# Window attention block on one core: K and Q projected ahead of the first MLP layer, their low parts taken ahead of x's statistics

## The chip, the cores and the metric

The kernel runs on one core of one Trainium2 chip. The metric is the time of one execution in microseconds (us) of device time. Names of engines: PE is TensorE (matmuls), PEld its weight loads, DVE is VectorE, ACT is ScalarE, POOL is GpSimd, SP is SyncE, which here only issues DMAs.

## The reference

One block of a Swin transformer on x of 32 images of 56 x 56 tokens with 128 channels, in float32: windows of 7 x 7 tokens, shifted by 3, 16 heads of 8 channels, an MLP with 512 hidden channels. Cut to what matters:

```
y = layernorm(x, norm1_g, norm1_b); y = roll(y, (-3, -3)); yw = windows of 7 x 7 tokens of y
q, k, v = split(yw @ qkv_w.T + qkv_b)              # 16 heads of 8
attn = softmax(q * 8**-0.5 @ k.T + bias + mask)     # bias by relative position, mask where the roll wraps
o = roll(attn @ v @ proj_w.T + proj_b, (3, 3))
x = x + o
h = layernorm(x, norm2_g, norm2_b)
out = x + gelu(h @ fc1_w.T + fc1_b) @ fc2_w.T + fc2_b
```

## The kernel before

A step of the work is a band of 7 rows of a pair of images: 16 windows, 784 tokens. There are 128 steps (`STEPS`), and the engines work through turns `t` of -2 to 130; each turn holds pieces of several steps, so that attention of step t, K, Q and maximum logits of step t + 1, statistics of x of step t + 2, the output projection of step t - 1, and the MLP of steps t - 2 and t - 3 share one turn. Nothing is scheduled by a tool: each engine's program is written out by hand in the order in which it runs, each instruction waits for semaphores, and a wait that is not yet met holds up all that stands behind it on that engine.

The order of a turn in which all pieces exist (t from 2 to 126), as far as the change and the prediction touch it:

- PE: transposes of z2 (L838, step t - 2) and of z1 (L846, step t + 1), the transpose of the maxima (L749), the first three token rows of the second MLP layer (`fc2(t - 3, 0, i)`, L821), chunks 0 and 1 of the first MLP layer (`fc1`, L805: six matmuls a chunk, into PSUM banks 2 and 3 or 4 and 5), K and then Q (L867: six matmuls each, K into banks 0 and 1, Q into banks 6 and 7), chunks 2 and 3 of fc1, the spread of the softmax reciprocals over channels (L881), V (L895, 24 matmuls), the output projection (L904), and then eight windows of logits (L771, L776), maximum logits (L741), attention times V (L791) and the rest of fc2.
- ACT: `h_hi` (L449), `yT_hi` (L464, four pieces), the table for gelu, gelu of chunks 0 and 1 (L438), `k_hi` and `q_hi` (L484), gelu of chunks 2 and 3, the table for exp, half of V (L500), then the exponentials (L421).
- DVE: `h_lo` (L600), the negated maxima (L607), `yT_lo` (L617, L621), reciprocals of the softmax sums (L630), `finish(t - 3, 0)` (L581), which frees bank 7, then `norm1(t + 2)` (statistics of x: seven at L521, seven at L527), `k_lo` and `q_lo` (L641), the division (L657), the other half of V (L672, L687), the residual (L681), the row maxima (L589).
- SP issues in this order: softmax sums, x of step t + 2 (L206), the attention's output, two pieces of the negated maxima (L246), the reciprocals' rows (L281), two more pieces of L246, the four `mx_k` (L296) and `mx_q` (L300) copies for the maximum logits, the output, 15 copies into `st_k` and `st_q` (L315, L318), x again for the residual.

Every f32 value that goes into a 16-bit matmul is split into a high part (a cast) and a low part (the difference), so K needs `yT_hi` and `yT_lo`, and `k_hi`, `k_lo` are made by ACT and DVE in turn from the same PSUM banks. The waits that matter:

```
pe.wait_ge(s_y_lo, n + 1)                            # ahead of K; n = t + 1
if bank == 6 and exists(t - 3):
    pe.wait_ge(s_fin, 2 * (t - 3) + 2)               # ahead of Q: finish(t - 3, 0) has read bank 7
pe.wait_ge(s_h_lo, n + 1)                            # fc1 chunk 0
pe.wait_ge(s_gelu, CH * n + c - 1)                   # fc1 chunk c = 2, 3: gelu of chunk c - 2 has read the banks
pe.wait_ge(s_lo, 2 * (t + 1) + 1)                    # spread: k_lo has read banks 0 and 1
pe.wait_ge(s_lo, 2 * (t + 2))                        # V: q_lo has read banks 6 and 7
dve.wait_ge(s_x, loads(n, edge(n)))                  # norm1: x of step t + 2 has landed
```

In the last turns (t of 127 and more) there is no step t + 1 any more, so K and Q are absent there, and from t = 126 on there is no `norm1`.

Of the kernel before, what the change touches and what calls it, by code (L numbers as in the profile page):

```python
# [71 lines left out]
def swin_block_kernel(nc, x, wqT, wkT, wvT, wvpT, wpT, w1T, w2T, cols, rows, table_k, table_q, ident, eye,  # L72
# [11 lines left out]
    with ctx:  # L84
# [63 lines left out]
        def tokens_of(bank):  # L148
            return ps[:, bank:bank + 2, :].rearrange("p b (i c) -> p (b i) c", c=C)
# [34 lines left out]
        def exists(n):  # L184
            return 0 <= n < STEPS

        def past(n, k):
            return n > k

        def loads(n, edge):  # L190
            return 64 * (n + 1) - 32 * EDGE if edge else 32 * (n + 1)
# [212 lines left out]
        @block.scalar  # L404
        def _(act):
            act.wait_ge(s_w, 16 * N_W)

            nc.scalar.mul(w_q, w_q, HD ** -0.5).then_inc(s_inita, 1)
            nc.scalar.mul(col[:, BQ:BQ + 1], col[:, BQ:BQ + 1], HD ** -0.5).then_inc(s_inita, 1)
            act.wait_ge(s_inita, 2)  # L410

            def load_table(function):

                nc.scalar.activation(scrap[:, :], col[0:1, 0:1], function)  # L414

            def exp_pair(n, w):
                if w >= 4 or past(n, 0):
                    act.wait_ge(s_pv, NU * n + w // 2 - 1)
                act.wait_ge(s_st, NW * n + w + 1)
                b = 2 + 2 * (w % 2)  # L420
                nc.scalar.activation(probs[0:KP, w % 4, :].rearrange("p (b c) -> p b c", b=2),  # L421
                                     ps[0:KP, b:b + 2, 0:HB * WT], ACT.Exp).then_inc(s_exp, 1)

            def copy_pv(n, u):
                act.wait_ge(s_pv, NU * n + u + 1)
                if u == 0 and past(n, 0):
                    act.wait_ge(s_o_dma, N_O * n)
                    act.wait_ge(s_sum_dma, N_SUM * n)
                nc.scalar.activation(pv_sb[:, :, 2 * u * WT:2 * (u + 1) * WT],  # L429
                                     ps[:, 6, 0:NG * 2 * WT].rearrange("p (g q) -> p g q", g=NG),  # L430
                                     ACT.Copy).then_inc(s_pv_sb, 1)

            def gelu(n, c):
                if c == 0 and past(n, 0):
                    act.wait_ge(s_fc2, 2 * n)
                act.wait_ge(s_fc1, CH * n + c + 1)
                bank = 2 + 2 * (c % 2)
                nc.scalar.activation(hid[:, c, :].rearrange("p (b q) -> p b q", b=2), ps[:, bank:bank + 2, 0:HT],  # L438
                                     ACT.Gelu, bias=col[:, BF + c:BF + c + 1], scale=1 / W_SCALE).then_inc(s_gelu, 1)

            def body(t, edge, odd):
                if exists(t - 1):
                    copy_pv(t - 1, NU - 1)
                n = t - 2
                if exists(n):
                    act.wait_ge(s_t2, n + 1)
                    if past(n, 0):
                        act.wait_ge(s_fc1, CH * n)
                    nc.scalar.activation(h_hi[:, :].rearrange("p (i c) -> p i c", c=TP),  # L449
                                         tokens_of(2)[:, 0:WS, 0:TP], ACT.Copy).then_inc(s_h_hi, 1)  # L450
                n = t + 1
                if exists(n):

                    act.wait_ge(s_t1, n + 1)
                    if past(n, 1):
                        act.wait_ge(s_v, 2 * (n - 1))
                    else:
                        act.wait_ge(s_initp, 1)
                    src = tokens_of(0)[:, 0:WS, 0:TP].rearrange("p i (m c) -> p i m c", m=2)
                    dst = yT_hi[odd(1)][:, :, :, 0:WT].rearrange("p w m (i j) -> p w m i j", i=WS)  # L460
                    last_w = NW - 1
                    kept = WS - SS
                    def put(o, a):
                        return nc.scalar.activation(o, a, ACT.Copy)  # L464
                    for im in range(2):
                        put(dst[:, 0:last_w, im, :, :].rearrange("p w i j -> p i w j"),
                            src[:, :, im, SS:SS + last_w * WS].rearrange("p i (w j) -> p i w j", j=WS))
                    put(dst[:, last_w, :, :, 0:kept].rearrange("p m i j -> p i m j"),
                        src[:, :, :, W - kept:W])
                    put(dst[:, last_w, :, :, kept:WS].rearrange("p m i j -> p i m j"),  # L470
                        src[:, :, :, 0:SS]).then_inc(s_y_hi, 1)
                if exists(t - 2):
                    load_table(ACT.Gelu)
                    gelu(t - 2, 0)
                    gelu(t - 2, 1)
                n = t + 1
                if exists(n):

                    if past(n, 0):
                        act.wait_ge(s_mx_dma, N_MX * n)  # L480
                        act.wait_ge(s_st_dma, N_ST * n)
                    for j, (hi, bank, b) in enumerate(((k_hi, 0, BK), (q_hi, 6, BQ))):
                        act.wait_ge(s_qk, 2 * n + j + 1)
                        nc.scalar.activation(hi[:, :, :, :].rearrange("p w m q -> p m w q"),  # L484
                                             ps[:, bank:bank + 2, 0:BT].rearrange("p m (w q) -> p m w q", w=NW),
                                             ACT.Identity, bias=col[:, b:b + 1]).then_inc(s_hi, 1)
                if exists(t - 2):
                    gelu(t - 2, 2)
                    gelu(t - 2, 3)
                if exists(t):  # L490
                    load_table(ACT.Exp)
                n = t
                if exists(n):
                    if past(n, 0):
                        act.wait_ge(s_pv, NU * n)
                    else:
                        act.wait_ge(s_init, 2)
                    for b in range(2):
                        act.wait_ge(s_v, 2 * n + b + 1)
                        nc.scalar.activation(v_place(1, b), v_made(1, b), ACT.Copy).then_inc(s_vown_b, 1)  # L500
                if exists(t):
                    for w in range(NW):
                        exp_pair(t, w)
                        if w % 2 == 0 and w > 0:
                            copy_pv(t, w // 2 - 1)

            turns(body)


        @block.vector  # L510
        def _(dve):
# [18 lines left out]
            def norm1(n, edge):  # L530
                dve.wait_ge(s_x, loads(n, edge(n)))
                if past(n, 0):
                    dve.wait_ge(s_z1, n)
                stats(x_in, st1, (0, WS)).then_inc(s_st1, 1)
                aggregate(n, st1, s_st1, mv1, s_ln1)
# [59 lines left out]
            def body(t, edge, odd):  # L595
                n = t - 2
# [4 lines left out]
                n = t  # L601
# [7 lines left out]
                n = t + 1  # L609
# [16 lines left out]
                n = t - 1  # L626
# [3 lines left out]
                    nc.vector.reciprocal(sums[:, :, :], sums[:, :, :]).then_inc(s_rsum, 1)  # L630
                if exists(t - 3):
                    finish(t - 3, 0, edge)
                n = t + 2
                if exists(n) and n != 0:
                    norm1(n, edge)
                n = t + 1
                if exists(n):
                    for j, (hi, lo, bank, b) in enumerate(((k_hi, k_lo, 0, BK), (q_hi, q_lo, 6, BQ))):
                        dve.wait_ge(s_hi, 2 * n + j + 1)
                        for im in range(2):  # L640
                            last = nc.vector.scalar_tensor_tensor(  # L641
                                lo[:, :, im, :], ps[:, bank + im, 0:BT].rearrange("p (w q) -> p w q", w=NW),
                                col[:, b:b + 1], hi[:, :, im, :], ALU.add, ALU.subtract)
                        last.then_inc(s_lo, 1)
                n = t - 1
                if exists(n):

# [18 lines left out]
                n = t  # L666
# [6 lines left out]
                n = t - 1  # L673
# [10 lines left out]
                n = t  # L684
# [3 lines left out]
                for w in range(NW):  # L688
                    if exists(t + 1):
                        row_maxima(t + 1, w)  # L690
                    n = t - 1
# [14 lines left out]
        def _(pe):  # L706
# [119 lines left out]
            def body(t, edge, odd):  # L826
                if exists(t - 1):
                    pv(t - 1, NU - 1)
                n = t - 2
# [10 lines left out]
                n = t + 1  # L840
# [9 lines left out]
                if exists(t - 3):  # L850
                    for i in range(*FC2_PARTS[0]):
                        fc2(t - 3, 0, i)
                if exists(t - 2):
                    fc1(t - 2, 0)
                    fc1(t - 2, 1)
                n = t + 1
                if exists(n):
                    pe.wait_ge(s_y_lo, n + 1)
                    high, low = ([y[odd(1)][:, :, im, 0:WT] for im in range(2)] for y in (yT_hi, yT_lo))
                    for w_hi, w_lo, bank in ((wk_hi, wk_lo, 0), (wq_hi, wq_lo, 6)):  # L860
# [6 lines left out]
                                last = mm(ps[:, bank + im, 0:BT], ww[:, :], yy[im], start=(k == 0), stop=(k == 2))  # L867
                        last.then_inc(s_qk, 1)
                if exists(t - 2):
                    fc1(t - 2, 2)  # L870
                    fc1(t - 2, 3)
                n = t - 1
# [11 lines left out]
                n = t  # L884
# [14 lines left out]
                n = t - 1  # L899
# [79 lines left out]
```

## Time and profile before

| | |
|---|---|
| median of 3 runs | 4095.21 us (4090.11 to 4104.3) |
| the profiled execution | 4095.41 us, span 4093.6 us |
| PE busy | 3947.3 us, 96% of the span |
| DVE, ACT, POOL busy | 70%, 65%, 49% |
| mean granted TensorE clock | 0.995 |

The span runs from the first to the last instruction of one profiled execution; the profiled execution's own time is 1.8 us more. A share of busy time is that of the whole span. Matmuls are pipelined, and the length shown for one (0.33 us for 392 columns) is more than the distance from one to the next (0.165 us); a group of two in the rows has one start, the next group's start tells the pace. A turn lasts some 31 us.

### The profile page before, as it was taken

Reading aid. Unit: us, or ns where it says so; the run is one execution under the profiler, and the core shown is the slowest. Engines: PE = TensorE matmul, PEld = TensorE weight load, DVE = VectorE, ACT = ScalarE, POOL = GpSimd, SP = SyncE. Lnnn points to the kernel's source line nnn. Section 1 sums busy time; section 2 is a strip of 40 time slices with the busy share of each in tenths; the row PEclk is TensorE's granted clock in tenths of the full one; section 3 lists DMA queues with packets and bytes.
Section 4 is the critical chain, followed back from the end, with each engine's and each line's share of the span. In section 5 each row is a group of like instructions: output and inputs, shape, how many; then the busy total and the mean of one; then the engine's idle time right before and its main releaser. Section 6 shows DMA issues by size and latency. Waiting matters only on the chain. (4 is left out here: it accounts for less than half of the span.)

```text
span 4093.6 us, 168809 instructions
## 1 busy us (share of the span) xinstructions
PE 3947.3 (96%) x72080; PEld 3111.1 (76%) x72080; DVE 2855.1 (70%) x7453; ACT 2674.9 (65%) x3712; POOL 2002.3 (49%) x3476
## 2 busy tenths in 40 slices
PE   3899999999999999999999999999999999999998
PEld 2677777777777777777777777777777777777776
DVE  6677677677767777776776776777777667677764
ACT  1666666666666666666766666666666666666664
POOL 4454545445455454544544544454454445445453
PEclk8999999999999999999999999999999999999999
DMA  2333333333333333333333333333333333333332
GB/s 77 100 108 115 109 109 112 110 105 112 114 106 110 113 111 110 111 113 105 112 114 105 110 114 110 109 111 108 108 109 117 106 109 112 112 105 109 112 109 60
DMA packets 609568, 441.49 MB, mean 108 GB/s; under 512 B 142083, under 2 KB 608371, under 8 KB 608819
## 3 DMA queue, kind: packets, MB, share of 16 engines
q1 hardware_dynamic: 608355, 428.88, 35.6%
q8 instruction: 569, 9.32, 1.0%
q0 software_dynamic: 464, 1.81, 0.2%
q14 instruction: 180, 1.47, 0.1%
HBM read 106.14 MB, written 51.46 MB: 38 GB/s over the span
## 5 line engine op out<-in xcount | busy, mean ns | idle before, releaser
L589 DVE TENSOR_REDUCE neg_max<-ps 113x16 f32<-113x784 f32 x1024 | 995.9, 973 | 760.7 <-PE ps L741 760.5
L421 ACT ACTIVATE probs<-ps 113x784 f32<-113x784 f32 x1024 | 844.6, 825 | 858.4 <-PE ps L776 855.7
L821 PE MATMUL ps<-w,hid 128*112 128x128 f32 x7168 | 933.5, 279 | 1.9 <-ACT hid L438 1.0
L821 PEld LDWEIGHTS ps<-w,hid 128*112 128x112 f32 x7168 | 818.4, 177 | 81.9 <-issue 79.4
L776 PE MATMUL ps<-st_q,st_k 128*49 128x196 f16 x8192 | 696.2, 249 | 0.0
L771 PE MATMUL ps<-bias,eye_k 106*64 106x392 f16 x4096 | 686.5, 331 | 0.0
L438 ACT ACTIVATE hid<-ps,col 128x784 f32<-128x784 f32 x512 | 468.1, 915 | 165.4 <-PE ps L805 144.2
L741 PE MATMUL ps<-mx_k,mx_q 128*49 128x196 f16 x8192 | 544.2, 253 | 31.7 <-DMA mx_q<-q_hi 20.0
L350 POOL TENSOR_SCALAR ve<-mv 112x7 f32<-112x7 f32 x256 | 54.4, 212 | 1048.4 <-DVE mv L527 903.1
L776 PEld LDWEIGHTS ps<-st_q,st_k 128*49 128x49 f16 x8192 | 446.9, 105 | 122.0 <-issue 0.5
L372 POOL TENSOR_SCALAR r_hi<-sums 128x98 f16<-128x98 f32 x128 | 36.5, 285 | 897.9 <-DVE sums L630 897.9
L791 PE MATMUL ps<-probs,v_own 113*32 113x49 f32 x32768 | 464.4, 209 | 1.8 <-issue 1.5
L791 PEld LDWEIGHTS ps<-probs,v_own 113*32 113x32 f32 x32768 | 393.2, 110 | 83.6 <-issue 82.8
L741 PEld LDWEIGHTS ps<-mx_k,mx_q 128*49 128x49 f16 x8192 | 313.1, 103 | 152.1 <-DMA mx_q<-q_hi 33.1
L361 POOL TENSOR_SCALAR x_in<-x_in,rs,nm 112x128 f32<-112x128 f32 x896 | 389.5, 451 | 13.5 <-POOL nm L356 0.4
L361 POOL TENSOR_SCALAR z<-x,rs,nm 112x128 f32<-112x128 f32 x896 | 388.5, 449 | 13.4 <-POOL nm L356 0.3
L352 POOL TENSOR_TENSOR rs<-ve,half 112x7 f32<-112x7 f32 x256 | 380.4, 1486 | 21.3
L429 ACT ACTIVATE pv_sb<-ps 128x392 f32<-128x392 f32 x512 | 255.6, 499 | 203.9 <-PE ps L791 192.4
L414 ACT ACT_TABLE_LOAD x253 | 324.6, 1283 | 4.5
L521 DVE BATCH_NORM_STATS2 st<-x_in 112x6 f32<-112x128 f32 x896 | 185.9, 279 | 201.8 <-DMA x_in<-in_x 201.8
L384 POOL TENSOR_TENSOR x_res<-x_res,proj_b 112x896 f32<-112x896 f32 x128 | 267.2, 2088 | 10.3
L391 POOL TENSOR_TENSOR x_b<-x,fc_b 112x896 f32<-112x896 f32 x128 | 267.1, 2087 | 5.6 <-DVE y_out L581 5.6
(109 smaller groups left out, 6502.4 us busy)
## 6 DMA issues: line engine op xcount, KB each, us to landing
st_k<-k_hi SPq DMA_DIRECT2D x256, 196.0 KB
st_q<-q_hi SPq DMA_DIRECT2D x1024, 49.0 KB
oT_raw<-pv_sb SPq DMA_DIRECT2D x256, 196.0 KB, 3.6
x_in<-in_x SPq DMA_DIRECT2D x224, 196.0 KB
x_res<-in_x SPq DMA_DIRECT2D x224, 196.0 KB
out_y<-y_out SPq DMA_DIRECT2D x224, 196.0 KB
mx_k<-k_hi SPq DMA_DIRECT2D x512, 49.0 KB
mx_q<-q_hi SPq DMA_DIRECT2D x128, 196.0 KB
```

Source lines behind the costliest of these rows:

```text
L352: nc.gpsimd.tensor_tensor(rs[:, :], ve[:, :], half[:, :], ALU.pow).then_inc(s_rs, 1)
L361: last = nc.gpsimd.tensor_scalar(z[:, i, :], src[:, i, :], rs[:, i:i + 1], nm[:, i:i + 1], ALU.mult, ALU.add)
L384: nc.gpsimd.tensor_tensor(x_res[:, :, :], x_res[:, :, :], proj_b[:, :].unsqueeze(1).to_broadcast([TP, WS, C]), ALU.add).then_inc(s_xres, 1)
L414: nc.scalar.activation(scrap[:, :], col[0:1, 0:1], function)
L421: nc.scalar.activation(probs[0:KP, w % 4, :].rearrange("p (b c) -> p b c", b=2), ps[0:KP, b:b + 2, 0:HB * WT], ACT.Exp).then_inc(s_exp, 1)
L438: nc.scalar.activation(hid[:, c, :].rearrange("p (b q) -> p b q", b=2), ps[:, bank:bank + 2, 0:HT], ACT.Gelu, bias=col[:, BF + c:BF + c + ...
L589: nc.vector.tensor_reduce(neg_max[0:KP, :, :, w].rearrange("p e g -> p g e"), ps[0:KP, 0:2, :].rearrange("p b (g c) -> p (b g) c", g=2)[:, ...
L741: last = mm(group(im, 0, g, 256), mx_q[edge(n)][:, g, span], mx_k[:, g, :, span], start=True, stop=True)
L771: mm(ps[HP * im:HP * (im + 1), bank + b, 0:HB * WT], eye_k[0:BIAS_ROWS, kind, im, :], bias[0:BIAS_ROWS, b, :], start=True, stop=False)
L776: last = mm(group(im, bank, g, EQ * WT), st_k[par][:, g, span], st_q[par][:, :, g, span], start=False, stop=(g % 2 == 1))
L791: last = mm(ps[32 * r:32 * r + VC, 6, first:first + WT], v_own[0:KP, w, h, :], probs[0:KP, w % 4, h * WT:(h + 1) * WT], start=True, stop=True)
L821: last = mm(ps[0:TP, 7, (i - first) * C:(i - first + 1) * C], hid[:, c, i * TP:(i + 1) * TP], w_2[:, c, :], start=(c == 0), stop=(c == CH ...
```

## The change

On PE, K and Q are computed ahead of all four chunks of fc1 and no longer between chunks 1 and 2. On ACT, `k_hi` and `q_hi` come ahead of all four gelus. On DVE, `k_lo` and `q_lo` come ahead of `norm1`. All waits stay with their instructions; no instruction is added or removed, and the orders on SP and POOL are the same as before.

```
--- before.py
+++ after.py
@@ scalar
                 if exists(t - 2):
                     load_table(ACT.Gelu)
-                    gelu(t - 2, 0)
-                    gelu(t - 2, 1)
                 n = t + 1
                 if exists(n):
...
                                              ACT.Identity, bias=col[:, b:b + 1]).then_inc(s_hi, 1)
                 if exists(t - 2):
+                    gelu(t - 2, 0)
+                    gelu(t - 2, 1)
                     gelu(t - 2, 2)
                     gelu(t - 2, 3)
@@ vector
                 if exists(t - 3):
                     finish(t - 3, 0, edge)
-                n = t + 2
-                if exists(n) and n != 0:
-                    norm1(n, edge)
                 n = t + 1
                 if exists(n):
                     for j, (hi, lo, bank, b) in enumerate(((k_hi, k_lo, 0, BK), (q_hi, q_lo, 6, BQ))):
...
                         last.then_inc(s_lo, 1)
+                n = t + 2
+                if exists(n) and n != 0:
+                    norm1(n, edge)
@@ tensor
                     for i in range(*FC2_PARTS[0]):
                         fc2(t - 3, 0, i)
-                if exists(t - 2):
-                    fc1(t - 2, 0)
-                    fc1(t - 2, 1)
                 n = t + 1
                 if exists(n):
                     pe.wait_ge(s_y_lo, n + 1)
...
                         last.then_inc(s_qk, 1)
                 if exists(t - 2):
+                    fc1(t - 2, 0)
+                    fc1(t - 2, 1)
                     fc1(t - 2, 2)
                     fc1(t - 2, 3)
```

PE, from the end of fc2's first part on, before (L867 is K and Q, L805 is fc1; what stands in brackets is the semaphore waited for):

```order
L821 MATMUL ps<-w,hid 112x128 x11
L805 MATMUL ps<-h_hi,w_hi 128x392 [waits h_low_ready]
L805 MATMUL ps<-h_hi,w_hi 128x392
L805 MATMUL ps<-h_lo,w_hi 128x392 x2
L805 MATMUL ps<-h_hi,w_lo 128x392 x2
L805 MATMUL ps<-h_hi,w_hi 128x392 [waits exp_done]
L805 MATMUL ps<-h_hi,w_hi 128x392
L805 MATMUL ps<-h_lo,w_hi 128x392 x2
L805 MATMUL ps<-h_hi,w_lo 128x392 x2
L867 MATMUL ps<-yT_hi,wk_hi 128x392 [waits y_low_ready]
```

PE at the same place of the changed kernel, whose line for K and Q is L864:

```order
L821 MATMUL ps<-w,hid 112x128 x11
L864 MATMUL ps<-yT_hi,wk_hi 128x392 [waits y_low_ready]
L864 MATMUL ps<-yT_hi,wk_hi 128x392
L864 MATMUL ps<-yT_lo,wk_hi 128x392 x2
L864 MATMUL ps<-yT_hi,wk_lo 128x392 x2
L864 MATMUL ps<-yT_hi,wq_hi 128x392 [waits y_ready,neg_maxT_ready]
L864 MATMUL ps<-yT_hi,wq_hi 128x392
L864 MATMUL ps<-yT_lo,wq_hi 128x392 x2
L864 MATMUL ps<-yT_hi,wq_lo 128x392 x2
L805 MATMUL ps<-h_hi,w_hi 128x392 [waits h_low_ready]
```

Chunks 0 and 1 of fc1, twelve matmuls, stood between fc2 and K; now K follows fc2, and all four chunks of fc1 follow Q without anything between chunk 1 and chunk 2.

DVE, from `finish` to the division, before:

```order
L581 TENSOR_TENSOR y_out<-ps,x_b 112x384 [waits fc2_done]
L521 BN_STATS st<-x_in 112x6 [waits z1_ready,x_loaded]
L521 BN_STATS st<-x_in 112x6 x6
L527 BN_AGGR mv<-st 112x2 [waits stats1_done]
L527 BN_AGGR mv<-st 112x2 x6
L641 SCALAR_TENSOR_TENSOR k_lo<-ps,col,k_hi 128x8x49 [waits qk_high_ready]
L641 SCALAR_TENSOR_TENSOR k_lo<-ps,col,k_hi 128x8x49
L641 SCALAR_TENSOR_TENSOR q_lo<-ps,col,q_hi 128x8x49 [waits qk_high_ready]
L641 SCALAR_TENSOR_TENSOR q_lo<-ps,col,q_hi 128x8x49
L657 TENSOR_TENSOR oT<-oT_raw,ps 128x7x49 [waits projected,r_spread,o_in]
```

DVE at the same place of the changed kernel, whose line for the low parts is L638:

```order
L581 TENSOR_TENSOR y_out<-ps,x_b 112x384 [waits fc2_done]
L638 SCALAR_TENSOR_TENSOR k_lo<-ps,col,k_hi 128x8x49 [waits qk_high_ready]
L638 SCALAR_TENSOR_TENSOR k_lo<-ps,col,k_hi 128x8x49
L638 SCALAR_TENSOR_TENSOR q_lo<-ps,col,q_hi 128x8x49 [waits qk_high_ready]
L638 SCALAR_TENSOR_TENSOR q_lo<-ps,col,q_hi 128x8x49
L521 BN_STATS st<-x_in 112x6 [waits z1_ready,x_loaded]
L521 BN_STATS st<-x_in 112x6 x6
L527 BN_AGGR mv<-st 112x2 [waits stats1_done]
L527 BN_AGGR mv<-st 112x2 x6
L657 TENSOR_TENSOR oT<-oT_raw,ps 128x7x49 [waits projected,r_spread,o_in]
```

The wait for x's load (`x_loaded`) stood ahead of the low parts and now stands behind them.

## Rows read from the trace of the kernel before

**Rows 1.** The page: busy time of the engines, and TensorE's granted clock in tenths.

```profile
PE 3947.3 (96%) x72080; PEld 3111.1 (76%) x72080; DVE 2855.1 (70%) x7453; ACT 2674.9 (65%) x3712; POOL 2002.3 (49%) x3476
PEclk8999999999999999999999999999999999999999
```

**Rows 2.** Waits: who waited for whom, us in total, times, longest.

```profile
PE ps L895 <- DVE q_lo L641: 24.2, 55, 2.2
PE ps L741 <- DMA mx_q<-q_hi: 20.0, 24, 4.3
PE ps L881 <- DVE k_lo L641: 14.5, 26, 2.8
PE ps L881 <- DMA r_rows<-r_lo: 2.0, 3, 0.9
DVE st L521 <- DMA x_in<-in_x: 201.8, 128, 2.8
DVE sums L630 <- DMA sums<-pv_sb: 4.6, 9, 1.2
```

**Rows 3.** Timeline of PE in one turn: start us, us, instructions.

```profile
1478.69 0.49 PE L805 MATMUL ps<-h_hi,w_hi 128*128 128x392 f16 x2
...
1480.68 0.50 PE L867 MATMUL ps<-yT_hi,wk_hi 128*128 128x392 f16 x2
...
1481.70 0.50 PE L867 MATMUL ps<-yT_hi,wq_hi 128*128 128x392 f16 x2
...
1482.72 0.49 PE L805 MATMUL ps<-h_hi,w_hi 128*128 128x392 f16 x2
...
1484.81 0.50 PE L881 MATMUL ps<-r_rows,sel 32*128 32x392 f16 x2
1485.24 0.23 PE L895 MATMUL ps<-wv_hi,yT_hi 128*128 128x128 f16 x1
...
1486.62 1.78 PE L904 MATMUL ps<-w_p,oT 128*112 128x128 f32 x14
```

**Rows 4.** Timeline of DVE and ACT in the same turn.

```profile
1478.32 0.34 DVE L621 TENSOR_TENSOR yT_lo<-ps,yT_hi 128x56 f16<-128x56 f32 x2
...
1479.22 0.50 DVE L581 TENSOR_TENSOR y_out<-ps,x_b 112x384 f32<-112x384 f32 x1
...
1484.02 1.15 DVE L641 SCALAR_TENSOR_TENSOR q_lo<-ps,col,q_hi 128x392 f16<-128x392 f32 x2
1485.40 1.16 DVE L657 TENSOR_TENSOR oT<-oT_raw,ps 128x343 f32<-128x343 f32 x4 [0.23 <-issue]
...
1477.35 1.28 ACT L414 ACT_TABLE_LOAD   x1
...
1479.95 1.85 ACT L438 ACTIVATE hid<-ps,col 128x784 f32<-128x784 f32 x2 [1.10 <-PE ps L805]
1481.98 0.93 ACT L484 ACTIVATE k_hi<-ps,col 128x784 f16<-128x784 f32 x1 [0.19 <-PE ps L867]
```

**Rows 5.** Timeline of DVE and PE in a turn with a late load of x.

```profile
2474.16 1.45 DVE L521 BATCH_NORM_STATS2 st<-x_in 112x6 f32<-112x128 f32 x7 [2.82 <-DMA x_in<-in_x]
...
2478.39 0.23 PE L895 MATMUL ps<-wv_hi,yT_hi 128*128 128x128 f16 x1 [0.49 <-DVE q_lo L641]
```

**Rows 6.** Timeline of PE's fc1 in a turn near the end, without K and Q.

```profile
4027.41 0.49 PE L805 MATMUL ps<-h_hi,w_hi 128*128 128x392 f16 x2
...
4029.63 0.51 PE L805 MATMUL ps<-h_hi,w_hi 128*128 128x392 f16 x2
```

**Rows 7.** Timeline of PE and DVE near the start, where K waited for yT_lo.

```profile
83.79 0.34 DVE L621 TENSOR_TENSOR yT_lo<-ps,yT_hi 128x56 f16<-128x56 f32 x2
...
84.19 0.84 PE L867 MATMUL ps<-yT_hi,wk_hi 128*128 128x392 f16 x2 [2.24 <-DVE yT_lo L621]
```

**Rows 8.** SP: its waits, and its timeline in the turn of rows 3.

```profile
SPq L294 <- ACT k_hi L484: 6.5, 2, 4.7
...
1483.54 2.92 SPq L296 DMA_DIRECT2D mx_k<-k_hi  x4
```

More of the change, by code:

```diff
@@ L473, in body @@
                     load_table(ACT.Gelu)
-                    gelu(t - 2, 0)
-                    gelu(t - 2, 1)
                 n = t + 1
@@ L487, in body @@
                 if exists(t - 2):
+                    gelu(t - 2, 0)
+                    gelu(t - 2, 1)
                     gelu(t - 2, 2)
@@ L632, in body @@
                     finish(t - 3, 0, edge)
-                n = t + 2
-                if exists(n) and n != 0:
-                    norm1(n, edge)
                 n = t + 1
@@ L644, in body @@
                         last.then_inc(s_lo, 1)
+                n = t + 2
+                if exists(n) and n != 0:
+                    norm1(n, edge)
                 n = t - 1
@@ L852, in body @@
                         fc2(t - 3, 0, i)
-                if exists(t - 2):
-                    fc1(t - 2, 0)
-                    fc1(t - 2, 1)
                 n = t + 1
@@ L869, in body @@
                 if exists(t - 2):
+                    fc1(t - 2, 0)
+                    fc1(t - 2, 1)
                     fc1(t - 2, 2)
```

## The prediction

> **What bounds the kernel now.** I read the page first: PE is busy 96% of the span, the next engine 70% [rows 1]. So only time in which PE waits, or is made to wait, counts. The view of waits says where the rest is: in the steady turns PE waits for `q_lo` ahead of V (24.2 us), for the copies of K and Q that the maximum logits need (20.0 us), for `k_lo` ahead of the spread (14.5 us) and for the rows of the reciprocals (2.0 us) [rows 2]. The first, third and last sum to 40.7 us; over the 125 turns in which all pieces exist (t = 2 to 126) that is 0.33 us a turn. This is all that the change can win at that place.
>
> Why PE waits there is seen in a turn with a late load [rows 5]. DVE stood 2.82 us in front of `norm1` until x landed; the low parts queued behind it, and V began 0.49 us late after a spread that was late too. DVE waits for that load in nearly every turn, 201.8 us in 128 [rows 2]; only where x is late enough does PE feel it. A turn with an early load shows the undisturbed pace [rows 3, 4]. I count its times from 1478.69, when fc2's first part is through and fc1 starts; call it 0. Then K starts at 1.99, Q at 3.01, chunk 2 of fc1 at 4.03, the spread at 6.12, V at 6.55, the projection at 7.93 [rows 3]. V is just not held up there: `q_lo` ends at 6.48 (1485.17). The other turns are late against this one by those 0.33 us on average.
>
> **The change, part by part.** No instruction is added or removed, so busy time stays and the sum is one of waits.
>
> *Removed.* `k_lo` and `q_lo` no longer stand behind `norm1` and its load, and they have both chunk pairs of fc1 as cover. The 24.2 and 14.5 us go: -38.7 us. If nothing else moved, the kernel would win 0.9%.
>
> *Added: K directly behind fc2.* Chunks 0 and 1 of fc1 took 1.99 us and covered the making of `yT_lo`. That ends at 1478.66 [rows 4], which is -0.03. The start of the kernel, where K did wait, shows that K's first matmul begins 0.06 us after `yT_lo` ends (84.13 to 84.19) [rows 7]. K thus starts at 0.03: +0.03 us. That is luck rather than cover: any lateness of `yT_lo` now counts in full.
>
> *Added: Q behind `finish`.* Q needs bank 7, which `finish(t - 3, 0)` reads until 1479.72, that is 1.03 [rows 4]. With 0.06 for the wake-up Q starts at 1.09, where K's end would allow 1.05 (K to Q is 1.02): +0.04 us. Chunk 0 of fc1 starts at 2.11.
>
> *Added: the four chunks in one piece.* Chunk 2 writes the banks that gelu 0 reads, and Q and K no longer stand between. The turns near the end have just this order: chunk 0 starts at 4027.41, chunk 2 at 4029.63, 2.22 us later where two chunks take 1.99 us [rows 3, 6]: +0.23 us. (The wait is gelu's length plus the delay from chunk 0's start to gelu's, 1.26 us by rows 3 and 4, against 1.99 us of matmuls.) Chunk 3 then waits for gelu 1, which ends some 0.94 us after gelu 0, while chunk 2 takes 1.0 us: nothing, or 0.02. So chunk 2 starts at 4.33, the spread 2.09 later [rows 3] at 6.42 to 6.44, and V another 0.43 later at 6.86.
>
> *Is DVE in time?* `k_hi` ends at 0.03 + 1.30 + 0.93 = 2.26, `q_hi` at 1.09 + 2.23 = 3.32, `q_lo` 1.15 later at 4.5 [rows 3, 4]. `norm1` follows, about 2.0 us (from its start to V 4.23 us, less two low parts of 1.1 each [rows 4, 5]). Its load has landed by then: the longest wait for x in the run is the 2.82 us of [rows 5], begun when `finish` was through, so at 1.03 + 2.82 = 3.85. `norm1` thus ends at 6.5, ahead of the division, which waits for the spread: 0.59 us from the spread's start to its own [rows 3, 4], 1.16 us for itself, 0.06 until the projection, 6.43 + 1.81 = 8.24 against 7.93. V's matmuls, 1.38 us at most [rows 3], end at 8.24 as well. **A changed turn is longer than the undisturbed one by 0.31 us**: 125 x 0.31 = +38.8 us.
>
> *The late sums.* DVE waits 4.6 us in nine turns for the sums ahead of the reciprocal [rows 2]. `finish` stands behind that, and Q now waits for `finish` without slack: up to +4.6 us. The 2.0 us for the reciprocals' rows stay.
>
> *SP and POOL.* Their orders don't change. SP reaches the copies of K at 1483.54, when `k_hi` (ended 1482.91) was done, and in the whole run it waited for `k_hi` only twice [rows 4, 8]. So an earlier K starts no transfer earlier: `mx_k`, `mx_q`, output and `st_k`, `st_q` leave at the same times within a turn, and the 20.0 us of waiting for `mx_q` are not won. In those 24 turns the landing sets the pace, and a V that is 0.31 us later costs nothing there, up to 24 x 0.31 = 7.4 us less. But in some of these the removed wait had been hidden in the same way, so I take nothing off and use the 7.4 us for the lower end. POOL's first normalization gets its statistics some 0.5 us later, far ahead of the next turn's transposes, which wait for it. ACT's last gelu ends 0.3 us later, and PE first waits for the exponentials behind it at the third window's logits; I take that as covered, and it is a part of rival B if it isn't.
>
> *ACT's table load.* It now stands right ahead of `k_hi`. It starts at 1477.35 and shows 1.28 us, and gelu 0 runs 2.60 us after the load's start, having waited for PE [rows 4]. `k_hi` would be asked for at 0.03 + 1.30 = 1.33 (1480.02), 1.39 us behind the load's end: by the rows it waits for nothing. The Trainium skill (ScalarE: Activation LUTs, "What ACT_TABLE_LOAD costs") says that a switch costs about 2.66 us, a drain included; an estimate by it frees ACT at 1480.01 with a small activation still ahead of `k_hi`, which would move `k_hi` by that one's length and gelu 0 by hundredths, about 2 us over the run. The row shows gelu at work earlier than that, so the row decides.
>
> **Sum.** -38.7 + 38.8 + 4.6 = +4.7 us, made against the profiled execution's own 4095.4 us, which is 0.2 us from the median: 4100 us. The expected gain is real, and is given back by three new small waits, the largest at chunk 2.
>
> **Rivals.**
> *A, as above, within 0.3%:* 4100 us, own range 4090 to 4108. Chance 0.66.
> *B, gelu comes late (slower).* By the sum `q_hi` ends at 1.09 + 1.30 + 0.93 = 3.32 and gelu 0 is asked for at 2.11 + 1.26 = 3.37: a margin of 0.05 us. Every 0.1 us by which K, `finish` or ACT is later than my readings moves chunk 2 of each turn by 0.1 us, 12.5 us over the run. With 0.15 us more a turn the time is 4119 us. It decides (over 0.3%) from 0.06 us a turn. For it speaks that three waits in series have no slack; against, that all of them recur with a constant length. Chance 0.18.
> *C, the copies profit (faster).* If K's and Q's copies landed earlier, the 20.0 us of [rows 2] would go too: 4080 us. Against it stands SP's order [rows 8]. Chance 0.06.
> *D, the new waits don't arise (faster).* Were PE's weight loads or the order of work able to hide the wait for gelu, 125 x 0.23 = 29 us would come off: 4071 us. The turns near the end speak against it. Chance 0.05.
> *E, the clock.* TensorE's granted clock is at the full level in all slices but the first [rows 1], with PE standing 2 us at a time in some turns [rows 2]. If more short halts took it to the lower level for fc1, K and Q, some 6 us of a turn would double, 750 us in all: 4850 us. The Trainium skill (TensorE: Matmul & The Clock Gate, "A second HAM failure mode: psum-queue depth-cycling") tells of a kernel whose frequent short halts between groups made the clock swing; by that rule this would be the case, but the trace doesn't bear it out, halts of this size are there already. Chance 0.01.
> *F, nothing at all moves,* since x mostly lands early enough: the removed 38.7 us are measured waits, so this ends where A ends. Chance 0.04.
>
> **Numbers.** What a measurement of this kernel can tell from no change is about 0.3%, 12 us. A's range lies mostly inside it; B reaches over it. The range from 4083 to 4117 us leaves out E, most of C and D, and the upper part of B, in all less than 2 in 10. Faster by over 0.3% 0.12 (C, D, a little of A), within 0.3% 0.68, slower 0.20 (B, E and the upper edge of A).
>
> **What will show it.** In the changed kernel's view of waits, `q_lo` ahead of V and `k_lo` ahead of the spread should be gone, DVE's wait for x in front of the statistics too (x landed while it made the low parts). PE's weight loads should wait for ACT's gelu ahead of L805 in nearly every turn. In a timeline, K should start within 0.1 us of fc2's end, chunk 2 should start 2.22 us after chunk 0, and the distance from fc2's end to V should be 6.86 us in nearly all turns, where it was 6.55 to 8. `mx_q` should be waited for as often as before. I am wrong if `yT_lo` or `finish` come later than here (K or Q start late), if chunk 2 waits for more than 0.3 us, or if the transfers change their times within a turn.

## The result: 0.4% slower, and the profile after

The changed kernel takes 4109.96 us (median of 9 runs, 4106.26 to 4116.73), the kernel before 4095.21 us (9 runs in the same comparison, 4084.42 to 4104.3). The ratio is 1.004, 95% interval 1.0028 to 1.0052: slower, by less than 15 us. The profiled execution has a span of 4104.5 us where the one before had 4093.6.

The first two rows are of the page of the changed kernel, the others of its view of waits:

```profile
PE 3994.1 (97%) x72080; PEld 3097.4 (75%) x72080; DVE 2857.1 (70%) x7453; ACT 2673.2 (65%) x3712; POOL 2002.2 (49%) x3476
PEclk9999999999999999999999999999999999999999
...
PEld ps L805 <- ACT hid L438: 79.6, 255, 0.8
...
PE ps L741 <- DMA mx_q<-q_hi: 7.3, 8, 4.5
PE ps L864 <- DVE y_out L581: 3.8, 10, 0.9
PE ps L880 <- DMA r_rows<-r_lo: 3.5, 3, 1.7
PE ps L894 <- DVE q_lo L638: 2.2, 1, 2.2
...
DVE st L521 <- DMA x_in<-in_x: 2.4, 1, 2.4
```

Against [rows 2]: V's wait for `q_lo` fell from 24.2 to 2.2 us, the spread's wait for `k_lo` is gone, and DVE stood before x's statistics for 2.4 us instead of 201.8. What the change is made for, it does. In its place PE's weight loads wait for ACT ahead of fc1, 255 times. PE's busy time rose by 47 us although it runs the same matmuls: short waits hide in it, since the length shown for a matmul (0.33 us) reaches beyond the start of the next (0.165 us later). The busy share says nothing here; the starts do.

Timeline of PE in an undisturbed turn of the changed kernel:

```profile
2105.99 0.51 PE L864 MATMUL ps<-yT_hi,wk_hi 128*128 128x392 f16 x2
...
2107.14 0.50 PE L864 MATMUL ps<-yT_hi,wq_hi 128*128 128x392 f16 x2
...
2108.16 0.49 PE L805 MATMUL ps<-h_hi,w_hi 128*128 128x392 f16 x2
...
2110.38 0.51 PE L805 MATMUL ps<-h_hi,w_hi 128*128 128x392 f16 x2
...
2112.48 0.50 PE L880 MATMUL ps<-r_rows,sel 32*128 32x392 f16 x2
2112.91 0.23 PE L894 MATMUL ps<-wv_hi,yT_hi 128*128 128x128 f16 x1
...
2114.29 1.78 PE L903 MATMUL ps<-w_p,oT 128*112 128x128 f32 x14
```

Timeline of DVE and ACT in the same turn:

```profile
2106.49 0.50 DVE L581 TENSOR_TENSOR y_out<-ps,x_b 112x384 f32<-112x384 f32 x1
2108.27 1.16 DVE L638 SCALAR_TENSOR_TENSOR k_lo<-ps,col,k_hi 128x392 f16<-128x392 f32 x2 [1.27 <-ACT k_hi L482]
2109.34 1.15 DVE L638 SCALAR_TENSOR_TENSOR q_lo<-ps,col,q_hi 128x392 f16<-128x392 f32 x2
2110.41 1.44 DVE L521 BATCH_NORM_STATS2 st<-x_in 112x6 f32<-112x128 f32 x7
...
2107.31 0.93 ACT L482 ACTIVATE k_hi<-ps,col 128x784 f16<-128x784 f32 x1 [1.19 <-PE ps L864]
2108.36 0.93 ACT L482 ACTIVATE q_hi<-ps,col 128x784 f16<-128x784 f32 x1
2109.41 1.85 ACT L438 ACTIVATE hid<-ps,col 128x784 f32<-128x784 f32 x2
2111.59 1.91 ACT L438 ACTIVATE hid<-ps,col 128x784 f32<-128x784 f32 x2 [0.33 <-PE ps L805]
2113.52 1.28 ACT L414 ACT_TABLE_LOAD   x1
2114.81 0.20 ACT L414 ACTIVATE scrap<-col 1x1 f32<-1x1 f32 x1
2115.02 2.12 ACT L500 ACTIVATE v_own<-ps 49x512 f32<-49x512 f32 x2
```

Counted from the end of fc2's first part (4.12 us after the turn's first transpose, here 2105.97), K starts at 0.02, Q at 1.17, chunk 0 at 2.19, chunk 2 at 4.41, the spread at 6.51, V at 6.94, the projection at 8.32. The undisturbed turn of before had V at 6.55 and the projection at 7.93 [rows 3]. For averages below I took the start of V in each of the 121 turns from 232 us to 3992 us, counted in the same way: 6.88 before, 6.99 in the changed kernel. In the changed kernel V starts within 0.03 us of 6.94 in 99 of these turns, and later than 7.0 in 17, at most at 7.90. Before, it started within 0.05 us of 6.55 in 42 turns, ahead of 6.93 in 83, and the latest was at 8.08. So most turns became longer, by up to 0.39 us, and the late ones became fewer.

Two averages behind V matter for the sum. From V to the first logits (L771) the changed kernel takes 3.10 us; before it was 3.09 us in an undisturbed turn, but 3.04 on average, since more than half of the turns took only 3.01 to 3.02 there. Why is not shown. The first logits thus start 0.17 us later than before on average (10.09 instead of 9.92), and 0.09 us of that is absorbed by the end of the turn.

### The profile page after: what moved, and what is told of

It reads as the page before. It is cut to its first block, busy times and chain, and to the rows that moved or that the text cites. A ratio compares the mean times of both kernels' runs of the same rounds, so it can differ in the third digit from the quotient of the medians.

```text
span 4104.5 us, 168809 instructions
## 1 busy us (share of the span) xinstructions
PE 3994.1 (97%) x72080; PEld 3097.4 (75%) x72080; DVE 2857.1 (70%) x7453; ACT 2673.2 (65%) x3712; POOL 2002.2 (49%) x3476
## 4 chain that ended last, share of the span: by engine, by line
PE 87%; SPq 3%; ACT 3%; DMA 2%; DVE 2%; issue 2%; POOL 0%; ACTq 0%; DVEq 0%; POOLq 0%
PE ps L821 20%; PE ps L741 12%; PE ps L791 10%; PE ps L805 9%; PE ps L776 9%; PE ps L771 9%; PE ps L864 6%; PE ps L903 5%; PE ps L894 4%; ACT hid L438 3%; PE ps L838 2%; PE ps L846 2%; PE ps L880 1%; SPq L296 1%; DMA mx_q<-q_hi 1%
## 5 line engine op out<-in xcount | busy, mean ns | idle before, releaser
L771 PE MATMUL ps<-bias,eye_k 106*64 106x392 f16 x4096 | 687.1, 331 | 0.0
L500 ACT ACTIVATE v_own<-ps 49x512 f32<-49x512 f32 x256 | 265.4, 1139 | 7.4 <-PE ps L894 5.7
```

What stands on the lines that cost most here:

```text
L771: mm(ps[HP * im:HP * (im + 1), bank + b, 0:HB * WT], eye_k[0:BIAS_ROWS, kind, im, :], bias[0:BIAS_ROWS, b, :], start=True, stop=False)
```

## The experiments

Times are medians; the kernel before ran beside them and had 4092.8 us in the first four, 4092.4 us in the others. The changed kernel's 4109.96 us is from the comparison above, where the kernel before had 4095.2 us, so a difference from it is good to some 3 us; the ratios to the kernel before are free of that.

### 1. What does Q wait for? `finish` ahead of the reciprocal

```
 (DVE, changed kernel)
+                if exists(t - 3):
+                    finish(t - 3, 0, edge)
                 n = t - 1
                 if exists(n):
                     dve.wait_ge(s_sum_dma, N_SUM * (n + 1))
                     nc.vector.reciprocal(sums[:, :, :], sums[:, :, :]).then_inc(s_rsum, 1)
-                if exists(t - 3):
-                    finish(t - 3, 0, edge)
```

> The changed kernel with one swap on DVE: the addition that frees PSUM bank 7 (finish, first part) ahead of the reciprocal instead of behind it. In the changed kernel Q's first matmul starts 1.14 us behind K's, where K's matmuls alone take 1.02; I had forecast 1.06. Theory (Q stands behind finish): the bank is free 0.65 us earlier, Q starts 1.02 to 1.04 us behind K, a turn is 0.10 to 0.12 us shorter, about 13 us less than the changed kernel (4097 us against 4110), less what the 0.5 us later reciprocals cost through SP's queue (mx_k and mx_q leave up to 0.5 us later). Rival (two waits in front of Q cost this time whether they are met or not): Q still starts 1.14 us behind K and the time is that of the changed kernel or more.

Measured: 4097.63 us (12 runs), 12.3 us less than the changed kernel; ratio to the kernel before 1.0007 (0.9996 to 1.0019). Timeline of PE and DVE:

```profile
2101.88 0.51 PE L864 MATMUL ps<-yT_hi,wk_hi 128*128 128x392 f16 x2
...
2102.91 0.50 PE L864 MATMUL ps<-yT_hi,wq_hi 128*128 128x392 f16 x2
...
2102.05 0.56 DVE L581 TENSOR_TENSOR y_out<-ps,x_b 112x384 f32<-112x384 f32 x1 [0.23 <-PE ps L821]
```

With bank 7 free at 2102.61, Q follows K after 1.03 us; in the changed kernel it was 1.15 (2105.99 to 2107.14). The rival falls: Q was held by `finish`. `mx_k` leaves 0.52 us later in this kernel on average, and the waits for `mx_q` rose from 7.3 to 15.0 us, yet the time fell by nearly all of the 13 us forecast. Both waits still stand ahead of Q here.

### 2. Does chunk 2 wait for gelu? Half-length gelus

```
 (ACT, changed kernel, in gelu)
+                nb = 1 if c < 2 else 2
-                nc.scalar.activation(hid[:, c, :]..., ps[:, bank:bank + 2, 0:HT],
+                nc.scalar.activation(hid[:, c, 0:nb * HT]..., ps[:, bank:bank + nb, 0:HT],
```

> The changed kernel with the gelus of chunks 0 and 1 done for the first half of their columns only (392 of 784; half of these two chunks' hidden values stays undone), so that each lasts some 0.6 us instead of 0.92. Theory (chunk 2 of the first MLP layer waits 0.23 us for gelu 0): chunk 2 starts 1.99 us behind chunk 0 instead of 2.22, chunk 3 another 1.0 us later, a turn is 0.25 us shorter, 31 us less than the changed kernel: 4079 us. Rival (the 0.23 us is not gelu's, but a cost of the order of the matmuls or of the weight loads): chunk 2 still starts 2.22 us behind chunk 0 and the time stays at 4110 us.

Measured: 4084.97 us (12 runs), 25 us less than the changed kernel; ratio to the kernel before 0.9978 (0.9966 to 0.999). The kernel leaves out half of the gelus of chunks 0 and 1, so its time is not one for the whole work. Timelines of PE and ACT:

```profile
2093.54 0.49 PE L806 MATMUL ps<-h_hi,w_hi 128*128 128x392 f16 x2
...
2095.53 0.49 PE L806 MATMUL ps<-h_hi,w_hi 128*128 128x392 f16 x2
...
2094.80 0.59 ACT L439 ACTIVATE hid<-ps,col 128x392 f32<-128x392 f32 x1
```

Chunk 2 starts 1.99 us behind chunk 0, as forecast, and the rival falls. V starts 0.25 us earlier on average, 31 us over 125 turns; 25 us of it reach the end. The waits for `mx_q` rose from 7.3 to 22.1 us in the profiles of the two: where that landing sets the pace, an earlier V only waits longer. That this is where the other 6 us went is likely, not shown.

### 3. The change on PE and ACT alone

The changed kernel with `norm1` back ahead of the low parts on DVE (the middle part of the diff undone).

> The change on PE and ACT alone; on DVE x's statistics stay ahead of the low parts, as before. Theory (the three new waits come from PE's and ACT's order, and DVE's order only decides whether a late x reaches PE): K, Q and the chunks start as in the changed kernel, but q_lo ends 4.2 us after x has landed, which in a quarter of the turns is later than the spread's end; V is 0.14 us later on average, 18 us over the changed kernel: about 4125 us, and the waits of V for q_lo are back in some 30 turns. Rival (DVE's order is what costs, for instance by the later statistics): the time falls below the changed kernel's 4110 us.

Measured: 4115.3 us (6 runs), ratio 1.0049 (1.0032 to 1.0065); 5 us above the changed kernel where 15 us were forecast, and the two intervals (the changed kernel's is 1.0028 to 1.0052) overlap. DVE waits for x again, 191.4 us, and V waits for `q_lo` in 15 turns (6.9 us), not 30. V starts at 7.05 of the turn on average, 0.06 us later than in the changed kernel. The waits came back as forecast, but at less than half the size. That DVE's half of the change wins time once K and Q are both early is not shown by these runs; if it does, it is little.

### 4. A version of my own: K first, Q left between chunks 1 and 2

```
 PE                          ACT                    DVE
 K                           k_hi                   reciprocal, finish
 fc1 chunks 0, 1             gelu 0, gelu 1         k_lo
 Q                           q_hi                   norm1(t + 2)
 fc1 chunks 2, 3             gelu 2, gelu 3         q_lo
 spread, V                                          division
```

> A version of my own: K ahead of the first MLP layer as in the change, but Q left between chunks 1 and 2 as before; ACT in the order k_hi, gelu 0, gelu 1, q_hi, gelu 2, gelu 3; on DVE k_lo, then x's statistics, then q_lo. Theory (the change loses by the gap between chunk 1 and chunk 2 being closed, and by Q standing right behind finish): chunk 2 follows Q without a wait, Q has chunks 0 and 1 as cover for finish, only K's 0.03 us is left; x's landing is waited for 1 us later in the turn than before, so V starts at 10.83 us of the turn on average (before 11.00, changed kernel 11.1) and the time is 4075 to 4080 us. Rival (x's landing reaches PE as much as before, or K's early place costs elsewhere): 4095 us or more.

Measured: 4069.77 us (6 runs), ratio 0.9947 (0.9929 to 0.9965): faster than both, by 23 us against the kernel before and some 40 us against the changed one, and 5 us below the time expected. Timelines of PE and DVE:

```profile
2086.54 0.51 PE L866 MATMUL ps<-yT_hi,wk_hi 128*128 128x392 f16 x2
...
2089.56 0.50 PE L866 MATMUL ps<-yT_hi,wq_hi 128*128 128x392 f16 x2
...
2090.59 0.49 PE L812 MATMUL ps<-h_hi,w_hi 128*128 128x392 f16 x2
...
2092.67 0.50 PE L892 MATMUL ps<-r_rows,sel 32*128 32x392 f16 x2
...
2088.81 1.16 DVE L641 SCALAR_TENSOR_TENSOR k_lo<-ps,col,k_hi 128x392 f16<-128x392 f32 x2 [1.28 <-ACT k_hi L478]
2089.89 1.44 DVE L526 BATCH_NORM_STATS2 st<-x_in 112x6 f32<-112x128 f32 x7
...
2091.86 1.13 DVE L641 SCALAR_TENSOR_TENSOR q_lo<-ps,col,q_hi 128x392 f16<-128x392 f32 x2
```

Nothing waits between K and the spread: 6.13 us, against 6.49 in the changed kernel (2105.99 to 2112.48). The statistics fill the time in which DVE would wait for `q_hi`, and begin 0.8 us later than before on average, late enough for nearly every landing of x. V starts at 6.60 on average.

### 5. The 0.08 us that were missing: one wait less ahead of Q

```
 (PE, changed kernel)
-                        if bank == 6 and exists(t):
-                            pe.wait_ge(s_negT, t + 1)
                         if bank == 6 and exists(t - 3):
                             pe.wait_ge(s_fin, 2 * (t - 3) + 2)
```

> The changed kernel with one of the two waits ahead of Q taken out: that for the negated maxima (DVE makes them ahead of yT_lo, for which K has waited already, so that nothing is left unguarded). In the changed kernel Q starts 0.14 us behind the end of finish, where every other waiting matmul starts 0.05 to 0.07 us behind what it waits for. Theory (the second wait instruction in front of Q costs 0.08 us, which my forecast lacked): Q starts 0.06 us behind finish, a turn is 0.08 us shorter, 10 us less than the changed kernel (4100 us against 4110). Rival (the 0.14 us is between the end of an addition that reads PSUM and PE, whatever PE waits for): Q still starts 0.14 us behind finish and the time stays at 4110 us.

Measured: 4098.4 us (12 runs), 11.6 us less than the changed kernel; ratio to the kernel before 1.0014 (1.0004 to 1.0024). Timelines of PE and DVE:

```profile
2100.54 0.51 PE L862 MATMUL ps<-yT_hi,wk_hi 128*128 128x392 f16 x2
...
2101.60 0.51 PE L862 MATMUL ps<-yT_hi,wq_hi 128*128 128x392 f16 x2
...
2101.05 0.49 DVE L581 TENSOR_TENSOR y_out<-ps,x_b 112x384 f32<-112x384 f32 x1
```

Q starts 0.06 us behind the end of `finish` (2101.54). In the changed kernel it is 0.15 us (2106.99 to 2107.14). The semaphore taken out had long been reached; having two waits instead of one still cost 0.08 to 0.09 us a turn. The rival falls.

What the second wait adds can be seen. The view of line 861 of the changed kernel, which is the wait for `finish`, has an instruction of PE's sequencer for weight loads (PEldq) of its own in 124 turns; in this experiment there is none. In the kernel before, line 877, the wait for `k_lo` ahead of the spread, has one too:

```profile
L861 PEldq EVENT_SEMAPHORE  x124: 51/51/51, 176.3 to 4008.5; - x124
...
L877 PEldq EVENT_SEMAPHORE  x126: 51/51/51, 117.6 to 4002.4; - x126
```

So of two waits one becomes an instruction of 51 ns, here the one that is met last, and the weight load with the other wait comes behind it. In experiment 1 the same instruction is there, but `finish` is done while K's matmuls still run, and Q starts 1.03 us behind K: then it costs nothing that can be seen. Whether the price would go if the two waits changed places, so that the one met last stood with the weight load, was not tested.

### 6. The change on DVE alone

> The change on DVE alone, PE and ACT in the order of before. Theory (the low parts can go ahead of x's statistics only because K and Q come earlier): k_lo and q_lo still wait for k_hi and q_hi and end at 10.6 us of the turn, the statistics follow until 12.65 us and hold up the division; the projection starts at 13.9 us instead of 12.4, and the time is about 4270 us. Rival (DVE's order alone wins the waits for q_lo and k_lo): V starts at 10.67 us in every turn and the time is about 4055 us.

Measured in one run: 4240.71 us, the profiled one, against 4092.4 us of the kernel before. Timelines of DVE and PE:

```profile
2178.99 1.15 DVE L638 SCALAR_TENSOR_TENSOR q_lo<-ps,col,q_hi 128x392 f16<-128x392 f32 x2
2180.06 1.44 DVE L521 BATCH_NORM_STATS2 st<-x_in 112x6 f32<-112x128 f32 x7
...
2182.02 1.13 DVE L657 TENSOR_TENSOR oT<-oT_raw,ps 128x343 f32<-128x343 f32 x4
...
2183.21 1.46 PE L904 MATMUL ps<-w_p,oT 128*112 128x128 f32 x11 [1.49 <-DVE oT L657]
```

V starts at 6.55 in nearly every turn, so the two waits are indeed won, and the projection pays 1.5 us for it. It is 30 us less than forecast: the division starts 1.96 us behind the statistics, which I had put at 2.05 with a start 0.1 us later, and the waits for `mx_q` fall from 20.0 to 5.1 us behind the later projection. The rival had V's start right and the time wrong.

### 7. K first, but x's statistics ahead of both low parts

> My version with K ahead of the first MLP layer and Q between chunks 1 and 2, but with x's statistics ahead of both low parts, as before the change. Theory (that version's 25 us come from DVE's order, which takes x's late landing off PE; K's early place is only what makes the order possible): q_lo ends 4.2 us after x has landed, V starts at 11.0 us of the turn on average, the time is that of the kernel before, 4090 to 4098 us. Rival (the early K is what wins): it stays at 4070 us.

Measured: 4091.54 us (12 runs), ratio 0.9991 (0.9978 to 1.0004): no change. PE waits for `q_lo` 18.9 us in 47 turns and for `k_lo` 5.8 us in 12: the waits of [rows 2] are back, if somewhat smaller. Against experiment 4 it differs in the place of `norm1` alone, and that is worth 22 us. The early K by itself wins nothing.

### 8. K first, and SP's copies of the maxima ahead of the reciprocals' rows

```
 (SP, version of experiment 4)
                     neg(n, (0, 1), odd(0))
+                    neg(n, (2, 3), odd(0))
 ...
-                n = t
-                if exists(n):
-                    neg(n, (2, 3), odd(0))
```

> My version with K first, and on SP all four copies of the negated maxima ahead of the reciprocals' rows, where SP stood idle for 0.4 us before. Theory (mx_k and mx_q leave when SP has come to them, not when K and Q are ready): they leave 0.4 to 0.5 us earlier in the turn, the maximum logits wait less for mx_q (0.1 us a turn before), while the reciprocals' rows land 0.8 us later but mostly still ahead of the spread: 4062 to 4067 us against 4070. Rival (the wait for mx_q comes from the load on the DMA queues, not from when the copies are issued, or the later rows hold up the spread): 4070 us or more.

Measured: 4078.94 us (8 runs), ratio 0.997 (0.9955 to 0.9986), 9 us more than experiment 4; the two intervals just overlap, so the size is uncertain. Two rows of its view of waits:

```profile
PE ps L890 <- DMA r_rows<-r_lo: 21.4, 32, 2.9
...
PE ps L746 <- DMA mx_q<-q_hi: 8.4, 8, 4.5
```

`mx_k` left only 0.2 us earlier on average (8.84 instead of 9.04 us after the turn's first transpose), and the reciprocals' rows landed 1.0 us later. The wait for `mx_q` fell from 14.1 to 8.4 us, and 21.4 us for the rows took its place, where experiment 4 had 3.8. V starts at 6.76 on average, where experiment 4 had 6.60. My theory was wrong in its last step: the rows had no such reserve. The first step held by less than half, 0.2 us of the 0.4 to 0.5 expected.

## Why the prediction was right, point by point

The range (4083 to 4117 us) held the time, and the likeliest value was 10 us low. The case that I held for likeliest, A, did not quite come: its own range ended at 4108 us, 2 us below the median. What came out, slower by a little over 0.3%, had a chance of 0.2. The waits of the forecast came where it put them; that its sum was this close is in part luck, since errors of both signs met in it, as is told below the list.

- *Removed, 38.7 us:* right for the waits. 2.2 of the 24.2 us stay, in one turn, and the 14.5 us are gone. But they were worth less than they show: between V and the first logits the kernel before was 0.06 us a turn quicker (3.04 against 3.10 us), which gives back some 7 us over the run.
- *K directly behind fc2, +0.03 us:* right, K starts at 0.02.
- *Q behind `finish`, +0.04 us:* this is the mis-sized term of the sum. The mechanism was right (experiment 1), but Q starts at 1.17, not at 1.09, +0.12 us: I took 0.06 us for the wake-up, read from a matmul with one wait, and Q has two (experiment 5). The difference is 0.08 x 125 = 10 us. Without it (experiment 5) the kernel is 6.0 us above the one before, where the sum had 4.7. The price stood in the trace of before, in the very turn of [rows 5], from which I read only the wait in front of V. The spread has two waits, V has one:

```profile
2476.14 1.13 DVE L641 SCALAR_TENSOR_TENSOR k_lo<-ps,col,k_hi 128x392 f16<-128x392 f32 x2
2477.19 1.15 DVE L641 SCALAR_TENSOR_TENSOR q_lo<-ps,col,q_hi 128x392 f16<-128x392 f32 x2
...
2477.42 0.49 PE L881 MATMUL ps<-r_rows,sel 32*128 32x392 f16 x2 [0.92 <-DVE k_lo L641]
```

  `k_lo` ends at 2477.27 and the spread starts 0.15 us later; `q_lo` ends at 2478.34 and V starts at 2478.39, 0.05 us later. The spread has this distance in 31 turns of the kernel before.
- *Four chunks in one piece, +0.23 us:* right to the hundredth. Chunk 2 starts 2.22 us behind chunk 0, and experiment 2 shows that it is gelu's length. The last turns of the kernel, which run the changed order already, were a sound place to read it [rows 6].
- *DVE in time:* right. `q_lo` ends at 2110.49, 4.5 us into the turn; the statistics are through before the division, and only one turn waits for x.
- *The turn:* an undisturbed one 0.31 us longer was forecast, 0.39 was measured (8.32 against 7.93).
- *The late sums:* right in kind. Q waits visibly for `finish` in ten turns, 3.8 us where up to 4.6 were forecast. The rows of the reciprocals, taken as unchanged at 2.0 us, were waited for 3.5 us.
- *SP:* right that an earlier K starts no copy earlier: `mx_k` leaves 9.03 us after the turn's first transpose in the changed kernel, 9.02 before. I said that `mx_q` would be waited for as often; its waits fell from 20.0 to 7.3 us in the profile. Part of the longer turns was absorbed there; the lower end had allowed for 7.4 us of it, and it was 12.7. The 0.09 us a turn that are absorbed behind the first logits come to 11 us.
- *ACT's table load:* the row decides here again. `k_hi` starts 1.32 us behind K's first matmul; before it was 1.30 [rows 3, 4]. The second load of the turn shows it better: it starts 0.02 us behind the end of the last gelu (2113.50), and `v_own` starts 1.50 us after the load's start, with a small activation between, where the Trainium skill (ScalarE: Activation LUTs, "What ACT_TABLE_LOAD costs") would have it at 2.66 us or later. No drain is seen there, neither ahead of the load nor behind it.
- *Rivals:* B came nearest, slower by waits in series and beyond the 0.06 us a turn from which it was to decide, but through a cost that I had not named; `q_hi` was in time for gelu 0, which starts 0.12 us behind the end of `q_hi`. C was ruled out by SP's order, D by experiment 2, and E did not come: the granted clock is at its full level in all slices, 0.997 on average, with the 255 waits for gelu added. The Trainium skill's account of a swinging clock (TensorE: Matmul & The Clock Gate, "A second HAM failure mode: psum-queue depth-cycling") is not met here.

How the errors met, as an estimate from the averages: V starts 0.11 us later, 13.6 us over 125 turns, where the forecast with the price of the two waits has 14.7. Up to the first logits another 7 us come on top, and 11 us are absorbed behind them. That leaves some 10 us, and the profiled span grew by 10.9. The medians differ by 14.8 us; the changed kernel's profiled execution was the quickest of its nine.

The large part of the answer is that the change took away waits of 0.31 us a turn on average, and put 0.39 us into the path of every turn. Experiment 4 keeps the first and avoids the second, and experiment 7 shows that its gain comes from the place of `norm1`, which the early K only makes possible.

## What to carry to other kernels

When a producer is moved earlier, ask what had stood between it and its inputs, and between the pieces that it used to separate: here K and Q were the cover for the gelu that had to free a chunk's banks, and the first chunks were the cover for `yT_lo` and `finish`. Move only the half that is needed (K), and leave the other (Q) where it separates. On the engine that waits for a load of uncertain arrival, put the wait behind everything that others wait for and that is ready by then, and use the time in which it would stand idle anyway. When a wait will be the last to be met at its new place, read its price from an instruction with the same number of waits.

## What was not expected of the hardware

A second wait ahead of a matmul is not free, even when it has long been met. With two, the matmul starts 0.15 us behind the end of the DVE instruction that it waits for (Q behind `finish` in all 124 turns of the changed kernel, the spread behind `k_lo` in 31 turns of the kernel before), with one 0.05 to 0.07 us. The trace shows where most of it goes: one of the two waits is an instruction of its own, 51 ns long, ahead of the weight load. It cost 11.6 us over the run at Q (experiment 5), and nothing that could be seen in experiment 1, where it was met while earlier matmuls still ran.
